# One routing group for the last eight tiles, and the order of POOL's side work in a fused attention and expert layer

## What is computed

```python
# attention: 16 heads of 8; each of the 64 sequences attends to its own 64 context rows
s = layer_norm(ctx, ln1_g, ln1_b);  t = layer_norm(_layernorm(x), ln2_g, ln2_b)
q, k, v = t @ Wq, s @ Wk, s @ Wv
x = x + tanh(g_xattn[0]) * (softmax(q k^T / sqrt(8)) v) @ Wfc
# experts: 8 routed ones of which each token takes 2, and a shared one
xf = _layernorm(x).reshape(4096, 128)
gates = sigmoid(xf @ Wg)
vals, idx = top_k(gates, 2);  vals = vals / vals.sum(-1)
shared = silu(xf @ Ws1) * (xf @ Ws3) @ Ws2
routed = sum over the 2 experts e of vals_e * ((silu(xf @ We1[e]) * (xf @ We3[e])) @ We2[e])
out = x + tanh(g_ffn[0]) * (shared + routed) / 3
```

## Time and profile before

| | us |
|---|---|
| median of the runs | 461.61 (461.47 to 463.53) |
| the profiled execution | 458.93 |
| its span, first to last instruction | 457.1 |
| PE busy | 359.4 (79%) |
| DVE busy | 344.0 (75%) |
| POOL busy | 279.4 (61%) |
| ACT busy | 264.9 (58%) |

### The profile page before, as it was taken

How to read it: one execution, slowest core, us unless ns; L and a number is a source line. 1 busy time by engine, 2 the same in 40 slices (tenths; PEclk the granted TensorE clock), 3 DMA queues, 4 the chain that set the end, 5 groups by cost and what they waited for, 6 DMA issues and landing times.

```text
span 457.1 us, 10667 instructions
## 1 busy us (share of the span) xinstructions
PE 359.4 (79%) x3718; PEld 269.3 (59%) x3718; DVE 344.0 (75%) x866; ACT 264.9 (58%) x601; POOL 279.4 (61%) x375
## 2 busy tenths in 40 slices
PE   0689999997998969899869710999999999999400
PEld 0356666665765647676658600777777777778300
DVE  2559999999999998998848820576777777777447
ACT  1257777776687746687656600355555555556244
POOL 3373666666379966888647773017777777777700
PEclk9999999999799988899979865799999999999855
DMA  4920699991001110000001155113236666541179
GB/s 110 275 77 3 261 375 377 391 385 41 13 27 49 36 48 25 27 25 26 25 23 42 49 217 165 52 52 94 93 95 231 232 231 230 210 184 52 47 264 298
DMA packets 39331, 62.36 MB, mean 136 GB/s; under 512 B 5936, under 2 KB 23344, under 8 KB 39280
## 3 DMA queue, kind: packets, MB, share of 16 engines
q1 hardware_dynamic: 32704, 51.12, 32.6%
q0 software_dynamic: 4992, 10.30, 6.7%
q10 hardware_dynamic: 1584, 0.27, 0.4%
HBM read 18.32 MB, written 31.56 MB: 109 GB/s over the span
## 4 chain that ended last, share of the span: by engine, by line
PE 41%; DVE 25%; issue 13%; POOL 13%; ACT 4%; DMA 3%; POOLq 0%; DVEq 0%; SPq 0%; ACTq 0%
POOL expert_rows L545 7%; PE ps L1215 6%; PE ps L1216 5%; PE ps L1217 5%; DVE row_max L935 5%; PE ps L1252 3%; DVE inv_sum L976 3%; PE ps L1158 3%; POOL token_sums L622 3%; PE ps L1112 3%; DVE norm L900 2%; PE ps L1240 2%; PE ps L1238 2%; PE ps L1239 2%; DVE x_sb L1061 2%
## 5 line engine op out<-in xcount | busy, mean ns | idle before, releaser
L622 POOL DMA_INDIRECT token_sums<-prob,y_at x92 | 94.5, 1027 | 60.7 <-DVE prob L1035 38.8
L545 POOL DMA_INDIRECT expert_rows<-c_sb,pos x64 | 64.3, 1005 | 16.9 <-issue 16.8
L587 POOL TENSOR_TENSOR k_mask<-k_st,head_mask 128x512 f32<-128x512 f32 x32 | 33.5, 1046 | 43.8 <-ACT k_st L695 43.6
L739 ACT ACTIVATE h_hi<-prob 128x512 fp32r<-128x512 f32 x62 | 38.3, 634 | 36.5 <-DVE prob L998 36.5
L732 ACT ACTIVATE probT<-ps 128x512 f32<-128x512 f32 x62 | 36.9, 598 | 30.6 <-PE ps L1217 27.0
L1112 PE MATMUL ps<-k_mask,qT 32*64 32x256 f32 x512 | 46.0, 431 | 9.4 <-DVE prob L941 7.7
L998 DVE TENSOR_TENSOR prob<-ps,probT 128x512 f32<-128x512 f32 x62 | 40.2, 684 | 13.9 <-ACT probT L732 10.9
L935 DVE TENSOR_REDUCE row_max<-ps 128x16 f32<-128x1024 f32 x32 | 38.9, 1216 | 11.0 <-PE ps L1112 10.9
L1003 DVE TENSOR_TENSOR h_lo<-prob,h_hi 128x512 fp32r<-128x512 f32 x62 | 40.5, 689 | 3.4 <-ACT h_hi L739 0.4
L1019 DVE TENSOR_TENSOR xT_lo<-ps,xT_hi 128x512 fp32r<-128x512 f32 x23 | 15.9, 692 | 35.9 <-ACT xT_hi L744 35.9
L703 ACT ACTIVATE probT<-ps 128x512 f32<-128x512 f32 x64 | 35.2, 595 | 10.5 <-PE ps L1158 10.4
(11 more groups left out here) (164 smaller groups left out, 977.1 us busy)
## 6 DMA issues: line engine op xcount, KB each, us to landing
expert_rows<-zeros SPq DMA_DIRECT2D x36, 520.0 KB, 5.2
c_sb<-expert_rows SPq DMA_DIRECT2D x23, 260.0 KB, 2.7
wbuf_hi<-w_hi SPq DMA_DIRECT2D x15, 384.0 KB, 2.9
wbuf_lo<-w_lo SPq DMA_DIRECT2D x15, 384.0 KB, 3.4
w_raw<-in_L_ffn_We_dram SPq DMA_DIRECT2D x24, 128.0 KB, 4.2
c_sb<-token_sums SPq DMA_DIRECT2D x8, 256.0 KB, 4.7
xT_lo<-token_sums SPq DMA_DIRECT2D x8, 256.0 KB, 4.9
out_dram<-x_sb SPq DMA_DIRECT2D x8, 256.0 KB, 4.9
```

The costliest lines, as they stand in the source:

```text
L545: pool.indirect_dma_start(out=xs, out_offset=bass.IndirectOffsetOnAxis(pos[:, k, i:i + 1], 0), in_=c_sb[:, i, :], in_offset=None).then_inc ...
L622: pool.indirect_dma_start(out=ys, out_offset=bass.IndirectOffsetOnAxis(y_at[:, s, k:k + 1], 0), in_=yrows[:, s % 2, k * D:(k + 1) * D], in ...
```

## The change

- The last two groups of four become one group of eight (tiles 24 to 31), done in units 0 and 1 (`TAIL_UNIT = 0`); its gate is no longer in step 34, its count not in 36, its places not in 37.
- Steps 33 to 37 follow each other with no unit in between; all units come after step 37. ScalarE's high part of unit 0 moves from after step 33 to the end of step 32 (the last piece of the diff is ScalarE's).
- POOL scatters one tile a step until step 37 (tiles 14 to 19 in steps 32 to 37, where it was tiles 14 to 23), tiles 20 to 23 in unit 0 and 24 to 31 in unit 1.
- The tables are made in four parts, in steps 0, 1, 2 and 3: the zeros and the row numbers; the scale of the row numbers, `nowhere`, the memsets and `carry`; the two affine selects and the starts of `begins`; the last three iotas.
- In steps without a scatter (4 to 17), POOL waits for the second norm's row of tile t - 4 before it makes the low weights.

```diff
-    GROUPS = [(0, 8), (8, 16), (16, 24), (24, 28), (28, 32)]
+    GROUPS = [(0, 8), (8, 16), (16, 24), (24, 32)]
...
-        def attention_steps(step, first, unit):
+        def attention_steps(step, first):
             for t in range(FIRST, LAST + 1):
                 step(t, t % 2)
                 if t == NT:
                     first()
-                if NT < t < LAST:
-                    unit(t - NT - 1)
-
-        EARLY = LAST - NT - 1
         def expert_units(unit):
-            for n in range(EARLY, UNITS):
+            for n in range(UNITS):
                 unit(n)
...
-        GATE_STEP = [14, 22, 30, 34, None]
-        COUNT_STEP = [16, 24, 32, 36, None]
-        RANK_STEP = [17, 25, 33, 37, None]
-        TAIL_UNIT = 4
+        GATE_STEP = [14, 22, 30, None]
+        COUNT_STEP = [16, 24, 32, None]
+        RANK_STEP = [17, 25, 33, None]
+        TAIL_UNIT = 0
...
-            return {NT: [14], NT + 1: [15], NT + 2: [16, 17], NT + 3: [18, 19], NT + 4: [20, 21],
-                    NT + 5: [22, 23]}.get(t, [])
+            return {NT: [14], NT + 1: [15], NT + 2: [16], NT + 3: [17], NT + 4: [18], NT + 5: [19]}.get(t, [])
...
-            def tables():
+            def tables(part):
...
+                i = t - 4
+                if within(i) and not scatter_tiles(t):
+                    pool.wait_ge(xn2_ready, i + 1)
                 if splits(t):
                     pool.wait_ge(w_hi_ready, t - WS_FROM + 1)
...
-                if t == 0:
-                    tables()
+                if 0 <= t < 4:
+                    tables(t)
...
                 if n == TAIL_UNIT:
-                    for i in range(24, 28):
+                    for i in range(20, 24):
                         scatter(i)
                 if n == TAIL_UNIT + 1:
-                    for i in range(28, 32):
+                    for i in range(24, 32):
                         scatter(i)
...
+            def first():
+                silu(0)
+                high(0)
             def unit(n):
-                if n == 0:
-                    high(0)
```

More of the change, by code:

```diff
@@ L637, in _ @@
                 scale_first(0, part)
-            attention_steps(step, lambda: None, unit)
+            attention_steps(step, lambda: None)
             expert_units(unit)
@@ L689, in step @@
                 if t in GATE_STEP:
+                    if t > NT:
+                        act.wait_ge(x2_ready, NT)
                     gate_exponentials(GATE_STEP.index(t))
@@ L779, in scale_sums @@
                     last.then_inc(scaled, 1)
-            attention_steps(step, lambda: silu(0), unit)
+            attention_steps(step, first)
             expert_units(unit)
@@ L1071, in _ @@
                 first_aggregates([i, i + 1])
-            attention_steps(step, lambda: hidden(0), unit)
+            attention_steps(step, lambda: hidden(0))
             expert_units(unit)
@@ L1287, in unit @@
                         turn_sums(n - 1)
-            attention_steps(step, first, unit)
+            attention_steps(step, first)
             expert_units(unit)
```

56 lines of the change are left out of this document (30 added, 26 removed).

## The result

The changed kernel takes 449.17 us, the median of four runs (447.84 to 450.45), against 461.62 us before: a ratio of 0.972, interval 0.9675 to 0.9767. The profiled execution took 447.97 us with a span of 446.2, 10.8 us less than the span before (457.05 less 446.23). Two of the four runs took 447.8 and 448.0, two 450.4 and 450.5; six more, further down, have a median of 450.93 us, which lies inside the range.

What follows compares the result with a forecast made beforehand. POOL's queue of scatters bounds the middle, and the loop through TensorE and ScalarE is the attention steps' next limit. 0.9 + 2.3 + 5.2 = 8.4 us off 461.6 gives 453.2 us, range 449.5 to 457.0.

Steps and rivals of the forecast that it cites:

- Tables, 0.9: Steps 0 to 3: tables in four parts let tile 2's key mask and scores start earlier, gaining 0.9 us.
- The median's 2.7 us: Median before lies 2.7 us above the profiled execution; forecast subtracts the gain from the median, 461.6 - 8.4.
- Low weights, 2.3: Steps 4 to 14: POOL's subtraction leaves DVE's normalisation, 0.21 us in each of eleven steps, 2.3 us.
- Rival A: The stall only moves; steps 4 to 14 stay at 5.74 us, kernel at 455.5 us; chance 0.12.
- Steps 15 to 17, nothing: There the subtraction isn't over a normalisation, or is already behind the row, so the low-weights wait gains nothing.
- The tail, 5.2 and 0: Steps 33 to 37 back to back gain 5.2 us; merging the last groups into one of eight costs nothing.
- Both go with the group: ScalarE's 1.28 us table load and TensorE's 3.47 us gate wait in step 34 go; counted under back-to-back steps.
- B: Bare steps 33 to 37 are bound by latency and POOL waits in them: 455.9 us; chance 0.12.
- C: The one group closes too late, POOL waits for its positions: slower, 466.9 us at position time 268; chance 0.05.
- D: No net change: TensorE's clock stays low while it catches up after step 37, about 461 us; chance 0.04.
- The slots' stretch: From the first slot to the end, 173 us, untouched by the change; should stay.
- E: Steps 18 to 31 shift and lose a stall or two, up to 3 us more: 450.2 us; chance 0.06.

Runs made afterwards that it cites:

- the kernel with 48 fills: Changed kernel, TensorE multiplying 48 times 128x512, results overwritten, behind unit 5's turn in its wait for the rows: 448.02 us.
- the fill from the start: Changed kernel, TensorE multiplying the identity by itself 46 times from about 1.7 us on, before the first rows: 450.65 us.
- 48 fills with the rounding moved: Changed kernel with 48 throwaway multiplications before the rows and ScalarE's rounding of unit 0's products behind step 33's copies: 448.6 us.
- the filled waits: Changed kernel, TensorE multiplying the identity by itself in four waits behind VectorE (steps 15, 23, 32, 33), results overwritten: 456.54 us.
- the filled waits, up to the rows: Changed kernel with four filled waits, unit 0's rounding behind step 33's copies, and 45 throwaway multiplications up to the rows: 454.77 us.

## Why the prediction was wrong

- **Tables, 0.9.** The place was right and the size was not. On the path it measured 1.09 (alone) to 1.28 us. In medians it measured 3.7 us alone and 2.65 when undone. The step that failed is "other work ended only 0.87 us before the scores ... So 0.87 us": I took the wait of one execution as its price. In most executions the clock falls behind that wait; filling it, with the mask as late as ever, gave 1.4 us. Of the three terms this is the one that the medians put far from its forecast (2.1 for 2.3, 4.8 for 5.2).
- **The median's 2.7 us.** "The median of the runs shown ... is 2.7 us above that execution; the forecast is 461.6 - 8.4": this carried the distance from the profile to the median through the change as if the change could not touch it. That distance was part of the cost, at least as far as the tables' wait makes it. The profile that I read shows an execution of the kind that 16 in 106 are. That the time fell below the range by 0.3 us and not just inside it hangs on which four runs were drawn: by the six later ones it is 450.93, inside the range, with a gain of 10.9 us where 8.4 were forecast.
- **Low weights, 2.3.** Right: 2.43 and 2.41. Rival A did not come: GpSimd idles 1.30 us ahead of the mask. In the eleven steps as the prediction counts them it is 2.22, since the last of them, step 15 here, lost 0.21. The floor is the one that step 16 showed, and it stays with the low weights all but left out; the rows above show it as the loop through TensorE and ScalarE. So a freed VectorE alone, with 4.7, was not the bound.
- **Steps 15 to 17, nothing.** Wrong by -0.75: -0.21 in step 15, -0.80 in step 16, +0.26 in step 17. In step 16 the key mask, with the steps earlier, now meets a routing instruction:

```profile
113.33 1.08 DVE L849 TENSOR_TENSOR chosen<-gate_tmp 128x64 f32<-128x64 f32 x1
```
```profile
113.24 1.04 POOL L586 TENSOR_TENSOR k_mask<-k_st,head_mask 128x512 f32<-128x512 f32 x1 [0.86 <-ACT k_st L699]
```

  It took 0.28 us before. The Trainium skill ("SBUF — State Buffer", Who interferes with whom) says that a VectorE instruction with two SBUF inputs contends with a GpSimd instruction that reads SBUF, and that the shared ports are an exclusive lock. The trace agrees: the 1.08 us end 0.13 us behind the mask. In other profiles the mask meets the running sum behind it instead (1.05 us in place of 0.29 in the kernel with 48 fills), and whether it meets either hangs on the clock. Where the clock fell 2.2 to 3.8 us behind the row maximum of step 15, the mask came later and met neither, and step 16 took 7.02 us (low weights alone; the tables in one piece; the fill from the start; 48 fills with the rounding moved). In the other profiles with short steps, where it fell 3.9 to 5.0 us behind that row maximum or not in that step, it took 7.69 to 7.92. Low weights alone show the loss of step 15, 0.22.
- **The tail, 5.2 and 0.** The sum was right (5.44 and 5.34 us) and its division wrong. The one group, costed at nothing, brings 3.3 us by itself, and the steps back to back bring 2.1 on top of it. The step that failed is "Both go with the group", said inside the term of the units: the 3.47 us were seen to belong to the group, and booked to the other edit. Rivals B and C did not come: no wait behind step 33, and the places come at 241.6, which is 246.6 on the clock of before (step 31 comes 4.95 us earlier); 247.5 was forecast. (C was set aside with "no wait in the trace is of that size", which passes over TensorE's own 19.71 us ahead of the rows; nothing came of it here.)
- **The clock as a rival.** D had it as a loss while TensorE catches up. It went the other way, and elsewhere. The slots' stretch, which "should stay", fell by 0.43 us, less than the 2.0 us by which the two profiles of the kernel before differ there; the two profiles with a filled wait whose clock stayed up are 2.2 to 2.7 us shorter there than the first of the changed kernel.
- **Steps 18 to 31.** E was named for them, and 1.57 us came in the first profile. The same instructions take 89.2 to 94.3 us over these profiles, and not in proportion to the clock: with no fall at all (the filled waits) 90.4, the lengthened step 23 included, and with one fall, from 119.5 to 126.4 us (the filled waits, up to the rows), 93.5. The change's own part in the 1.57 I can't tell from the execution's. **Open** is also why two of the first four runs, and none of the six of the repeat, have the higher clock; the one fall that only the second profile has, at 214.1, goes with 1.6 us from step 31 to the first rows.

## What to carry to other kernels

Where an unchanged kernel's executions are spread more widely than the terms that one forecasts, look first at which of them the profile shows: a median above the profiled execution can be a cost with a place, and the change may remove it or not. A short wait of TensorE is priced by itself and by what the clock does behind it; filling it with work that is thrown away tells the two apart, if the fill is counted in instructions as the trace lists them. And when one wait stands in the way of two edits at once, undo one of them before dividing the gain.

## What the runs showed of the hardware that I had not expected

- TensorE's granted clock fell behind the wait for step 2's mask, 1.18 to 1.74 us long, in four profiles, and stayed up in the two where that wait was 0.87 us and the clock had risen only at 31.3 and 31.6 us. Where it had risen at 28.1 to 30.8 us and there was no such wait, or a filled one, it stayed. The Trainium skill ("TensorE: Matmul & The Clock Gate", What's actually happening) says that what watches the activity runs free of the kernel's start, so that the point of a change varies from run to run; the first rise here lies anywhere from 28.1 to 31.6 us with nearly the same work ahead of it. (The record of the clock begins with that rise; that it was at half before, the eight turns show, 1.92 us at 26.5 and 1.04 at 39.7 in the profile of before.)
- Ahead of the rows, fills that left 0.65 and 1.35 us of waiting kept the clock up; behind one that left 2.49 us it fell. But with 0.56 us left it fell too, 2.4 us behind the rows, so the length of the gap alone doesn't decide.
- 46 products of the identity, from the start on, raised the clock at 7.1 us instead of some 30, and it was lost again from 20.7 to 27.6: here the early rise was worth nothing (450.65 us), with the next waits still there.
